# Gated slot attention: both products with the running states cut into two halves, with a projection between the halves

## The reference, cut to what matters

```python
q, k, v = silu(x @ Wq.T), silu(x @ Wk.T), silu(x @ Wv.T)
f = log_sigmoid(x @ Wf.T) / 8;  s = 1 - exp(f);  g = exp(f)
# pass 1, per time step:  S1 = S1 * g[None, :] + outer(k, s);   ok = q @ S1
qv = softmax(ok)
# pass 2, per time step:  S2 = S2 * g[:, None] + outer(s, v);   ov = qv @ S2
o = silu(ov);  y = (o * rsqrt(mean(o * o) + eps) * g_w) @ Wo.T
x = x + y
```

## Time and profile before

| what | value |
|---|---|
| median of 3 runs | 3980.67 us (3979.2 to 3991.87) |
| the profiled execution, its time | 4001.88 us |
| the profiled execution, its span | 4000.2 us |
| mean granted TensorE clock in it | 0.913 of full speed |
| TensorE busy in the span | 87% |

### The profile page before, as it was taken

How to read it: one execution, slowest core, us unless ns; L and a number is a source line. 1 busy time by engine, 2 the same in 40 slices (tenths; PEclk the granted TensorE clock), 3 DMA queues, 4 the chain that set the end, 5 groups by cost and what they waited for, 6 DMA issues and landing times. The chain is left out here.

```text
span 4000.2 us, 89053 instructions
## 1 busy us (share of the span) xinstructions
PE 3474.7 (87%) x30432; PEld 2146.5 (54%) x30527; DVE 2738.3 (68%) x7206; ACT 2302.9 (58%) x5551; POOL 2101.4 (53%) x2183
## 2 busy tenths in 40 slices
PE   5999999967687999999999999984967885987678
PEld 1333333316683565656565665664955764765456
DVE  6888888856445777777777777755446874655465
ACT  2777777754234666666666666652337762764367
POOL 3333333316545777777777677757432332754275
PEclk8999999985797999999999999985979997988879
DMA  5433334302452121212222222222633332110001
GB/s 102 62 60 61 61 59 61 60 6 79 147 180 55 46 58 48 56 48 54 49 53 49 56 51 51 50 56 62 199 104 83 92 81 47 43 45 5 1 1 43
DMA packets 417473, 252.23 MB, mean 63 GB/s; under 512 B 251442, under 2 KB 344610, under 8 KB 415874
## 3 DMA queue, kind: packets, MB, share of 16 engines
q1 hardware_dynamic: 406340, 224.36, 24.0%
q0 software_dynamic: 10688, 22.17, 1.8%
HBM read 75.12 MB, written 41.75 MB: 29 GB/s over the span
## 5 line engine op out<-in xcount | busy, mean ns | idle before, releaser
L2545 POOL TENSOR_TENSOR ra_prob<-ra_prob,ra_inverse 128x256 f32<-128x256 f32 (+3 forms) x512 | 632.0, 1257 | 366.5 <-DVE ra_inverse L2761 364.7
L2354 DVE TENSOR_REDUCE ca_mx<-ca_ps_s 128x2 f32<-128x1024 f32 x512 | 600.6, 1211 | 117.2 <-PE ca_ps_s L2226 116.8
L2690 ACT ACTIVATE ra_prob<-ra_ps_s,ra_low 128x128 f32<-128x128 f32 (+3 forms) x1024 | 534.5, 532 | 241.6 <-DVE ra_low L2741 241.6
L2291 ACT ACTIVATE ca_pT<-ca_ps_p 128x512 f32<-128x512 f32 x1024 | 544.8, 599 | 203.9 <-PE ca_ps_p L2236 179.5
L2741 DVE CUSTOM_DVE_ANT_0 ra_ps_s<-ra_ps_s,ra_mask 128x128 f32<-128x128 f32 (+3 forms) x1024 | 480.2, 511 | 44.8 <-PE ra_ps_s L2638 44.4
L2226 PE MATMUL ca_ps_s<-ca_kst,ca_qst 128*128 128x512 bf16 x991 | 380.4, 389 | 32.8 <-DVE ca_mx L2354 14.3
L2696 ACT COPY ra_probT<-ra_ps_t 128x512 f32<-128x512 f32 x384 | 227.3, 592 | 257.1 <-PE ra_ps_t L2584 257.1
L2236 PE MATMUL ca_ps_p<-ca_qst,ca_kst 128*128 128x512 bf16 x962 | 362.8, 382 | 5.9 <-ACT ca_pT L2291 4.8
L2584 PE MATMUL ra_ps_t<-ident,ra_prob 128*128 128x128 f32 x2560 | 350.2, 276 | 2.7 <-ACT ra_probT L2696 1.3
L2638 PE MATMUL ra_ps_s<-ra_kz,ra_qz 64*128 64x128 f32 (+3 forms) x2048 | 348.2, 458 | 3.8 <-DMA ra_kz<-ra_rot 2.8
L2538 POOL TENSOR_TENSOR ra_rot<-ra_prod 128x512 f32<-128x512 f32 x256 | 321.4, 1278 | 44.0 <-DVE ra_prod L2750 44.0
(11 more groups left out here) (414 smaller groups left out, 7222.6 us busy)
## 6 DMA issues: line engine op xcount, KB each, us to landing
moe_w_own<-moe_w1T SPq DMA_DIRECT2D x142, 256.0 KB
ra_qz<-ra_rot SPq DMA_DIRECT2D x512, 64.0 KB, 2.0
ra_kz<-ra_rot SPq DMA_DIRECT2D x512, 64.0 KB, 2.0
ca_kst<-ca_bounce SPq DMA_DIRECT2D x256, 64.0 KB
ca_bounce<-ca_thirds SPq DMA_DIRECT2D x192, 64.0 KB, 2.8
ca_qst<-ca_bounce SPq DMA_DIRECT2D x64, 192.0 KB
moe_hs<-moe_rows SPq DMA_DIRECT2D x142, 66.0 KB
moe_raw<-in_L_ffn_W SPq DMA_DIRECT2D x32, 256.0 KB, 3.0
```

What stands on the lines that cost most here:

```text
L2291: nc.scalar.activation(pT[:, (NS * hp + u) % PRING, :], ps_p[n % NP][:], ACT.Exp).then_inc(sg["drained"], 1)
L2354: nc.vector.tensor_reduce(mx[:, hm % 2, 2 * j:2 * j + 2], ps_s[m % 2][:].rearrange("p (b k) -> p b k", b=2), AX.X, ALU.max)\
L2545: nc.gpsimd.tensor_tensor(at, at, inverse[:, n % PROB, 2 * tile:2 * tile + 2].unsqueeze(2).broadcast_to([P, 2, keys]), ALU.mult)\
L2690: nc.scalar.activation(prob[:, n % PROB, tile, head, 0:keys], part(n, tile)[:, head, :], ACT.Exp, bias=low[:, n % PROB, at:at + 1], scale= ...
```

## The change: what it does

Three groups of instructions are moved; none is added or removed.

- `before` now takes the blocks that it is to do, and returns its last instruction. Each of its two calls becomes two: blocks 1 to 7 (28 products), and blocks 8 to 15 (32 products), and the signal (`o1_in`, `o2_in`) comes from the second.
- Between the halves of the first stands the projection v, which stood behind the whole of it. Between the halves of the second stands the projection y, which stood between `inside(ps_o1)` and `sums(vx)`.
- On VectorE the addition of y to `X` moves from before `okT` to behind `f` and ahead of the scan `s2`.

```diff
-                def before(out, state, queries, signal):
-
-                    for n in range(1, NBK):
+                def before(out, state, queries, blocks_of):
+
+                    for n in blocks_of:
...
-                    last.then_inc(sg[signal], 1)
+                    return last
...
-                    if live(i5):
-                        need(pe, "o_done", i5)
-                        need(pe, "kT_ready", i1)
-                        need(pe, "added", i5 - 1)
-                        for c in range(TC):
-                            last = nc.tensor.matmul(ps_m[:, c * P:(c + 1) * P], oT[:, c * P:(c + 1) * P], wT[:, 4, :], start=True, stop=True)
-                        last.then_inc(sg["y_in"], 1)
...
-                        before(ps_o1, lambda n: s1T[:, n - 1, :], qm[:, i3 % 3], "o1_in")
+                        before(ps_o1, lambda n: s1T[:, n - 1, :], qm[:, i3 % 3], range(1, NBK // 2))
                     if live(i1):
                         need(pe, "qn_ready", i1)
                         for c in range(TC):
                             last = nc.tensor.matmul(ps_q[:, c * P:(c + 1) * P], xT[:, c * P:(c + 1) * P], wT[:, 2, :], start=True, stop=True)
                         last.then_inc(sg["v_in"], 1)
+                    if live(i3):
+                        before(ps_o1, lambda n: s1T[:, n - 1, :], qm[:, i3 % 3], range(NBK // 2, NBK)).then_inc(sg["o1_in"], 1)
...
-                        before(ps_o2, lambda n: s2[:, :, n - 1], q2m, "o2_in")
+                        before(ps_o2, lambda n: s2[:, :, n - 1], q2m, range(1, NBK // 2))
+                    if live(i5):
+                        need(pe, "o_done", i5)
+                        need(pe, "kT_ready", i1)
+                        need(pe, "added", i5 - 1)
+                        for c in range(TC):
+                            last = nc.tensor.matmul(ps_m[:, c * P:(c + 1) * P], oT[:, c * P:(c + 1) * P], wT[:, 4, :], start=True, stop=True)
+                        last.then_inc(sg["y_in"], 1)
+                    if live(i4):
+                        before(ps_o2, lambda n: s2[:, :, n - 1], q2m, range(NBK // 2, NBK)).then_inc(sg["o2_in"], 1)
...
-                    if live(i5):
-                        need(dve, "y_in", i5)
-                        need(dve, "ors_done", i5)
-                        for c in range(TC):
-                            xc = X[:, i5 * TC + c, :]
-                            last = nc.vector.scalar_tensor_tensor(xc, ps_m[:, c * P:(c + 1) * P], ors[:, c:c + 1], xc, ALU.mult, ALU.add)
-                        last.then_inc(sg["added"], 1)
...
                         nc.vector.scalar_tensor_tensor(f[:], ps_z[:], 0.0, zl[:], ALU.min, ALU.subtract).then_inc(sg["f_done"], 1)
+                    if live(i5):
+                        need(dve, "y_in", i5)
+                        need(dve, "ors_done", i5)
+                        for c in range(TC):
+                            xc = X[:, i5 * TC + c, :]
+                            last = nc.vector.scalar_tensor_tensor(xc, ps_m[:, c * P:(c + 1) * P], ors[:, c:c + 1], xc, ALU.mult, ALU.add)
+                        last.then_inc(sg["added"], 1)
```

More of the change, by code:

```diff
@@ L1684, in body @@
                         inside(ps_o1, bn, am1x).then_inc(sg["in1_in"], 1)
-                    if live(i5):
-                        need(pe, "o_done", i5)
-                        need(pe, "kT_ready", i1)
-                        need(pe, "added", i5 - 1)
-                        for c in range(TC):
-                            last = nc.tensor.matmul(ps_m[:, c * P:(c + 1) * P], oT[:, c * P:(c + 1) * P], wT[:, 4, :], start=True, stop=True)
-                        last.then_inc(sg["y_in"], 1)
-                    if live(i3):
                         need(pe, "vx_landed", i3, EXPAND)
```

## The result

| | before | after |
|---|---|---|
| median of 5 runs each on the same chip | 3982.06 us (3979.2 to 3991.87) | 4001.16 us (3999.05 to 4008.61) |
| ratio, 95% interval | | 1.0047, 1.0035 to 1.0058 |
| span of the profiled execution | 4000.2 us | 4006.9 us |
| mean granted TensorE clock in it | 0.913 | 0.914 |

The change makes the kernel slower by 19.1 us (4001.16 us); 22.1 us were forecast (4003 us). First the order of TensorE in a step without a stop, from one a2 to the next (start, us, ..., [idle before <- releaser]). It answers to the earlier trace rows.

The account below looks back on a forecast made before the run. The step was taken as a TensorE-VectorE relay, with q2m DMA waits before a2 also binding. Terms 17.9 + 1.0 + 0.2 + 1.2 + 1.8 = 22.1 us, added to 3980.67, gave 4003 us, range 3992 to 4016.

Parts of the forecast that it names:

- The wait of ors for the addition: GpSimd's ors waits for the addition now behind f, delaying the q2m DMAs and a2: 1.24 us lost per step.
- okT 0.25 us later: With v between the first run's halves, TensorE's turn of okT comes 0.17 to 0.32 us later, taken as 0.25.
- 17.9 us for twelve steps: Twelve full steps with i5, i3 and i1 live, each 1.49 us longer, 20.75 to 22.24 us.
- y hidden in the wait for qv: Between okT and qv, TensorE's own work grows to 4.83 us, under 5.18: y is covered, 0.35 us to spare.
- oT and osq 1.1 us later, harmless: o2_in, then oT on ScalarE and osq on GpSimd, about 1.1 us later; early enough in steps without stops.
- Steps with a stop, taken at nothing: Where TensorE stops inside a run, gains at okT and 0.1 us lost at qv were cancelled to zero.
- Entry (+1.2): First step with i3 loses 1.0 us to v on the path; the second, which has a stop, 0.2.
- late steps (+1.2): Two late steps with neither f nor v lose 0.6 us each, 1.2 us in all.
- The last two steps (+1.8): At the end, y before the second run's end costs 1.1 us; with ors waiting for the addition, 1.8.
- The stops: TensorE's "issue" idles inside product runs, 14.4 us in 12 stops, cost under 6 us over 12 steps; mostly covered.
- the blocks of 256 instructions: Skill's rule that 16 KiB instruction fetches are mostly hidden; said not to hold here, given stops of 1.10 and 1.75 us.
- The rival with the lower clock: TensorE idling more lowers its clock at a2: 12 us more, 4015 to 4022; chance 0.15, shared with whole stops.

## Why the prediction was right, point by point

- **The wait of ors for the addition (1.24 us a step).** Right, and it decided: 5.36 us from f to a2 where 5.23 were worked out, and without that wait the loss is gone (0.9999). Loss measured in the step shown: 5.36 - 3.99 = 1.37. Over the twelve steps the way from f to a2 grew from 4.03 to 5.32 us in the mean, 1.29 a step, 15.5 us in all. (The 4.03 has in it one wait of 2.04 us for a q2m DMA.)
- **okT 0.25 us later.** Half right. The turn came at 8.40 us instead of 8.26, a delay of 0.14, but it cost nothing in the step shown: the turn of qv is at 13.44 us after a2 in both kernels. The prediction said that VectorE's softmax chain from okT sets qv. The runs with v behind and with the carry moved show that var does, by the carry on GpSimd. Where var falls behind the carry, as in the steps shown, qv stands at about 13.4 us after a2 with okT turned at 7.76 or at 8.40, so these 0.6 us are free. What v between the halves costs in all is not shown.
- **Missing: f comes sooner.** In the step shown it took 16.33 us from a2 to f, not 16.76, where the prediction added 0.25. bT is 0.84 us shorter because osq now runs behind it; q2T and the sum of squares follow sooner, by 0.43 us in the end. Together: 1.37 - 0.43 = 0.94 us instead of 1.49. But osq held bT or shift in only five of the twelve steps of the kernel before. Over all twelve the way from a2 to f fell from 205.86 to 201.29 us: 1.7 of these 4.6 us in those five steps, and 2.9 in the other seven, which all had a stop in the kernel before, three of them at a granted clock of 0.92 to 0.94. This is the term of the sum that was mis-sized: +0.25 us a step forecast from a2 to f, -0.38 measured, and so 17.9 us for twelve steps, 10.9 measured. What part of the 2.9 us is the cuts and what part the clock is open.
- **y hidden in the wait for qv.** Right: 4.83 us of TensorE's own work were forecast from okT to qv; they are 3112.83 - 3107.79 - 0.24 = 4.80 us, and 0.24 us of wait is left.
- **oT and osq 1.1 us later, harmless.** Only half right, and for a reason that was not seen: the table load waits for y. In the changed kernel the sum of squares comes at 15.15 us after a2, just as osq ends, so what comes on top costs in full: in the kernel with y behind, oT and the sum of squares are both 1.01 us later.
- **Steps with a stop, taken at nothing.** Not right in sum, as just told: these steps gave time back. Single ones did the opposite: the worst of the changed kernel takes 3166.84 - 3142.85 = 23.99 us. In it a stop falls into the second half of the first run and another into y itself:

```profile
3151.12 0.45 PE L1672 MATMUL gsa_ps_o<-gsa_qm,gsa_s1T 128*32 128x32 f32 x29 [0.92 <-issue]
3152.38 0.65 PE L1638 MATMUL gsa_ps_t<-ident,gsa_okT 128*128 128x128 f32 x4 [0.81 <-DVE gsa_okT L1912]
...
3156.63 0.60 PE L1714 MATMUL gsa_ps_m<-gsa_wT,gsa_oT 128*128 128x128 f32 x3 [0.98 <-issue]
```

- **Entry (+1.2) and late steps (+1.2).** The first was too dear: +1.2 forecast, about nothing measured. Of this, 1.0 was for v on the path in the first step with i3, but there TensorE waited 5.18 us for qv in the kernel before and 4.32 in the changed one, and that wait took v up. In the first late step ors started 1.35 us after ovar instead of 0.25, and 0.1 us came back at the front instead of 0.5: +1.0 instead of +0.6. In the second, which took +1.9, a stop of 1.70 us falls where before one of 1.04 did.
- **The last two steps (+1.8).** Too low, +3.8. TensorE and VectorE at the end:

```profile
3374.30 1.78 PE L1714 MATMUL gsa_ps_m<-gsa_wT,gsa_oT 128*128 128x128 f32 x8
...
3379.06 1.87 PE L1731 MATMUL gsa_ps_t<-ones,gsa_osq 128*128 128x1 f32 x8 [1.83 <-POOL gsa_osq L1856]
3382.32 0.98 PE L1714 MATMUL gsa_ps_m<-gsa_wT,gsa_oT 128*128 128x128 f32 x3 [1.39 <-DVE X L1972]
```

```profile
3381.05 1.12 DVE L1972 SCALAR_TENSOR_TENSOR X<-gsa_ps_m,gsa_ors,X 128x128 f32<-128x128 f32 x4
```

  The y before the last now takes 1.7 us at the lower clock inside the second run, where before it lay in the wait for am2x. The last y waits 1.39 us for the addition before it, because both use `ps_m` and that addition now stands behind ovar. The prediction counted the wait of ors there (+1.8 in all) but not this one.
- **The stops.** The claim that they cost under 6 us in all agrees with the runs. With osq behind bT and both runs whole, eleven of the twelve steps take together 2.6 us more than eleven times the 20.26 us of a step without a stop; the twelfth, 23.19 us, has a stop and then a granted clock of 0.85. And the changed kernel without the wait of ors has few stops and is no faster than the kernel before (0.9999). The prediction also says that the blocks of 256 instructions do not hold here because there are stops. That does not follow. The traces show stops at fixed instructions: in the step of the earlier trace rows there are 30 and 67 products left, in the kernel before and in all four others with its order of TensorE. From the one stop to the other it is 30 + 8 + 4 + 32 + 53 = 127 matmuls, with their weight loads 254 instructions, and 127 again in the next step, where 8 and 45 are left (8 + 8 + 4 + 32 + 75). That is close to 256, and the profile leaves waits uncounted. Our reading, not shown by an experiment, is that the blocks are there and that crossing them is not hidden in these runs. In the changed kernel the order is another, and one such stop falls into y. Nothing was run to cause or cure a stop at a border, so the cause stays open.
- **The rival with the lower clock.** It did not come: the granted clock over the twelve steps is 0.98 in the kernel before and 0.99 in the changed one, though TensorE waits 1.4 us more before a2.

So direction and mechanism held, and the total of 22.1 against 19.1 us is good partly by luck, because two errors cancel: the full steps and the entry 8 us too dear, the late steps and the end 3.7 us too cheap.

## What to carry to other kernels

Before an instruction is moved, look up who waits for the signal that it gives, and then what stands behind that waiter in its own queue: here an addition that nobody needed held back four columns on GpSimd, and two DMAs behind them on which TensorE stood. Such a wait is often one on a buffer and not on data; a second buffer of four columns took it away and gave 0.48% back (1.0047 against 0.9999). A stall that the profile shows is worth its length only where no later wait covers it, and a step has to be measured from its start to the last wait in it to see that.

## What the runs showed of the hardware

- **VectorE stands while GpSimd works on SBUF.** bT, a product of two SBUF tiles on VectorE, takes 0.69 us alone and 1.53 beside osq; var, an operation on 128x4, takes 0.17 us alone and 0.62, 0.76, 1.23 and 1.28 beside the carry. Each time var ends 0.02 to 0.03 us after the carry does, whenever it began, so it is held until the carry is done and not slowed. The small shift behind bT, with two SBUF inputs, takes 0.15 us alone and 1.00 beside osq. The Trainium skill (SBUF — State Buffer, Who interferes with whom) has it so: a VectorE instruction with two SBUF inputs contends with a GpSimd instruction that reads SBUF, and one in a two-port mode takes turns with GpSimd, each blocking the other for a whole instruction. The trace agrees; var has one input, and whether it ran in a two-port mode no run here shows. q2T, whose other input is in PSUM, keeps its 0.69 us beside an osq of 3113.45 to 3114.49 in the changed kernel (it starts at 3113.53).
- **A table load waits with its activation.** The load ahead of oT takes 1.28 us and starts only when y is done, for which oT has to wait: 0.91 us of idle time ahead of it in the changed kernel, 1.91 with y behind, none with two buffers. It does not stand behind every wait of oT: in the changed kernel it starts at 3111.48, while the second run, for which oT waits too, goes on to 3112.59. Once the wait for y is the last, the load comes on top of it. The Trainium skill (ScalarE: Activation LUTs, What ACT_TABLE_LOAD costs) gives about 1283 ns for the load, as here, and 1380 ns of drain beside it; here the activation starts 0.01 us after the load ends, so no such drain shows.
